# Attention state gathered in the second result bank and scaled out by VectorE

## The reference

```python
x = x + tanh(g_xattn) * mlstm(layernorm(x), ctx, ctx, Wi, bi, Wf, bf, ln_scale)
x = x + tanh(g_ffn) * moe(layernorm(x), ...)        # top 2 of 16 experts, and a shared one

def mlstm(q, k, v, Wi, bi, Wf, bf, ln_scale):       # b=16, s=256, e=512, nh=16, dh=32
    ig, fg = gates of concat([q, k, v])             # (b, nh, s, 1)
    log_f_cum = [0, cumsum(log_sigmoid(fg))]
    log_D = where(ltr, log_f_cum[1:] - log_f_cum[1:].T, -inf) + ig.T
    max_log_D = max(log_D, axis=-1)
    D = exp(log_D - max_log_D)
    C = (q @ k.T / sqrt(dh)) * D
    normalizer = maximum(abs(C.sum(-1)), exp(-max_log_D))
    h = (C / (normalizer + 1e-6)) @ v
    return (h - mean(h)) * rsqrt(var(h) + 1e-6) * ln_scale      # per head of 32
```

## Time and profile before

| | |
|---|---|
| median of 3 runs | 920.21 us (920.08 to 920.5) |
| the profiled execution | 923.91 us, of which the span of the instructions 922.2 us |
| PE busy | 740.1 us, 80% of the span |
| DVE, POOL, ACT busy | 571.1, 441.7, 410.6 us |
| attention stage | from about 106 us to 340 us of the span |

### The profile page before, as it was taken

The page is one execution under the profiler, slowest core; times in us unless marked ns, Lnnn a source line. Parts: engine busy times, 40 slices in busy tenths (PEclk is TensorE's granted clock), DMA queues, the critical chain, the costliest instruction groups (busy, mean ns, idle before and its releaser), DMA issues.

```text
span 922.2 us, 21232 instructions
## 1 busy us (share of the span) xinstructions
PE 740.1 (80%) x7464; PEld 631.7 (68%) x7464; DVE 571.1 (62%) x1144; ACT 410.6 (45%) x817; POOL 441.7 (48%) x652
## 2 busy tenths in 40 slices
PE   1772399999999947802999979999999999698892
PEld 1441167667666636602999969999999998697881
DVE  4763556766766769687556645565565554575765
ACT  1764256666666634531222225565656655212110
POOL 2111247777777751153888851111112112677884
PEclk9987579999999977955999999999999999899997
DMA  8861454543543219002341034777767745334342
GB/s 274 262 230 32 138 170 133 162 121 129 160 130 124 85 54 390 17 1 93 150 161 58 0 111 142 246 233 237 246 217 253 238 141 186 108 118 160 114 140 78
DMA packets 91311, 139.31 MB, mean 151 GB/s; under 512 B 17322, under 2 KB 44714, under 8 KB 91264
## 3 DMA queue, kind: packets, MB, share of 16 engines
q1 hardware_dynamic: 71648, 111.41, 36.6%
q0 software_dynamic: 10240, 16.82, 5.7%
q10 hardware_dynamic: 9376, 10.49, 3.5%
HBM read 103.66 MB, written 43.38 MB: 159 GB/s over the span
## 4 chain that ended last, share of the span: by engine, by line
PE 33%; POOL 12%; issue 5%; DVE 2%; ACT 1%; DMA 1%; POOLq 0%; DVEq 0%; ACTq 0%
PE f_psH L1301 21%; PE f_psY L1323 10%; POOL w13l L1575 3%; POOL w13h L1575 3%; PE f_psT L1278 3%; POOL f_hl L1557 2%; POOL disp L1565 2%; POOL idle L1552 1%; DVE xres L1475 1%; DMA yexp<-ystage 1%; DVE f_xrows L1411 0%; DVE f_xl L1427 0%; ACT f_xh L1347 0%; DVE w2l L1434 0%; DVE f_w2l L1434 0%
## 5 line engine op out<-in xcount | busy, mean ns | idle before, releaser
L1557 POOL TENSOR_TENSOR f_hl<-f_hh 128x256 fp32r<-128x256 f32 (+1 forms) x96 | 73.9, 777 | 197.5 <-ACT f_hh L1365 197.0
L1301 PE MATMUL f_psH<-f_xh,f_w13h 128*128 128x256 f32 (+1 forms) x384 | 111.4, 290 | 2.7 <-DVE f_xl L1427 2.4
L1301 PE MATMUL f_psH<-f_xh,w13h 128*128 128x256 f32 (+1 forms) x384 | 109.9, 286 | 2.4 <-DVE f_xl L1427 2.4
L1301 PE MATMUL f_psH<-f_xh,f_w13l 128*128 128x256 f32 (+1 forms) x384 | 110.1, 287 | 0.0
L1301 PE MATMUL f_psH<-f_xl,f_w13h 128*128 128x256 f32 (+1 forms) x384 | 109.8, 286 | 0.0
L1301 PE MATMUL f_psH<-f_xh,w13l 128*128 128x256 f32 (+1 forms) x384 | 108.8, 283 | 0.0
L1301 PE MATMUL f_psH<-f_xl,w13h 128*128 128x256 f32 (+1 forms) x384 | 108.5, 283 | 0.0
L1360 ACT ACTIVATE f_sg<-f_psH 128x256 f32<-128x256 f32 (+1 forms) x96 | 36.1, 379 | 152.5 <-PE f_psH L1301 141.7
L738 ACT ACTIVATE dec<-ring 128x512 f32<-128x512 f32 x128 | 76.5, 597 | 45.4 <-PE ring L645 41.8
L1365 ACT ACTIVATE f_hh<-f_hh 128x256 fp32r<-128x256 f32 (+1 forms) x96 | 39.6, 413 | 113.5 <-DVE f_hh L1447 113.2
L1447 DVE TENSOR_TENSOR f_hh<-f_sg,f_psH 128x256 f32<-128x256 f32 (+1 forms) x96 | 39.4, 415 | 78.9 <-ACT f_sg L1360 70.0
(11 more groups left out here) (221 smaller groups left out, 1920.2 us busy)
## 6 DMA issues: line engine op xcount, KB each, us to landing
raw<-w13T SPq DMA_DIRECT2D x64, 352.0 KB, 3.9
gcT<-ctxT ACTq DMA_DIRECT2D x8, 1024.0 KB, 6.7
kT<-ctxT SPq DMA_DIRECT2D x16, 512.0 KB, 5.4
qst<-qT_all SPq DMA_DIRECT2D x16, 512.0 KB, 6.2
ctxs<-ctx SPq DMA_DIRECT2D x16, 512.0 KB, 3.4
disp<-zeros SPq DMA_DIRECT2D x4, 2048.0 KB, 17.6
raw<-w2T SPq DMA_DIRECT2D x16, 512.0 KB, 4.2
f_xrows<-disp SPq DMA_DIRECT2D x16, 512.0 KB, 5.1
```

The costliest lines, as they stand in the source:

```text
L1301: last = nc.tensor.matmul(psH[m][0:n, v, :], w[wp][:, c, col:col + n], x[xp][:, c, :], start=(c == 0 and p == 0), stop=(c == DC - 1 and p ...
L1557: nc.gpsimd.tensor_tensor(hs[r % 2][1][0:n, m, :], hh[0:n, m, :], hs[r % 2][0][0:n, m, :].bitcast(F32), ALU.subtract).then_inc(s["hl_ready ...
```

## The change

The state no longer goes through a ring bank. `gather_state` writes it to psO's second bank, columns 264 to 391, beside the results, and stands between D2 and D3 in place of behind `values`; it waits for `o_taken` of the result two steps back. VectorE copies and scales it out (four instructions, `keep_state`), between `take` and `residual` of the even step ahead of it, and counts up `state_taken`, for which `back` waits. ScalarE has no `keep_state`, and its `root` stands behind `keep_output` in place of ahead of it. The ring has 20 uses in a loop round where it had 22, and its bank turns are new: in an odd step D0 of the next step now follows D3's bank, and not that of `values`. GpSimd's `keys` waits for the new counter, and its `lift_values` of first chunks now waits by itself for the `values` that read them.

```diff
-        USES = 22
-        FIRST = (2, 6, 12, 17, 23, 28, 34)
-        LAST2, OUT, STATE = 0, 2, 3
+        USES = 20
+        FIRST = (2, 6, 11, 16, 21, 26, 31)
+        LAST2, OUT = 0, 2
 
         def next2(r):
-            return 3 + r % 2 if r > 0 else 2
+            return 3 if r > 0 else 2
...
-            def gather_state(i, r, out):
+            def gather_state(i, r):
                 b = batch(i, r)
                 pe.wait_ge(kk_ready, b + 1)
                 pe.wait_ge(v_ready, 2 * b + 1)
+                if r >= 2:
+                    pe.wait_ge(o_taken, 4 * i + r - 1)
                 for gg in range(4):
                     for k in range(4):
                         h = 4 * gg + k
-                        last = nc.tensor.matmul(out[32 * k:32 * k + 32, gg * DH:(gg + 1) * DH], kkw[:, h, :],
+                        last = nc.tensor.matmul(psO[32 * k:32 * k + 32, 1, 264 + gg * DH:264 + (gg + 1) * DH], kkw[:, h, :],
                                                 vals[:, 0, h, :], start=True, stop=True)
-                last.then_inc(filled, 1)
+                last.then_inc(state_done, 1)
 
             def back(i, r, out_use):
...
+                pe.wait_ge(state_taken, batch(i, r) + 1)
...
                     decay(i, r, 2 + k, bank(r, LAST2 + k))
+                    if r % 2 == 1 and k == 0:
+                        gather_state(i, r)
...
-                if r % 2 == 1:
-                    ring_free(use(STATE))
-                    gather_state(i, r, bank(r, STATE))
...
-                pe.wait_ge(emptied, uses(i, r, STATE) + 1)
-                values(i, r, bank(r, STATE + 1))
-                back(i, r, uses(i, r, STATE + 1))
+                pe.wait_ge(emptied, uses(i, r, OUT))
+                values(i, r, bank(r, OUT + 1))
+                back(i, r, uses(i, r, OUT + 1))
...
+                if r >= 1:
+                    keep_output(use(OUT), bank(r, OUT))
                 if r >= 2:
                     root(i, r - 2)
-                if r >= 1:
-                    keep_output(use(OUT), bank(r, OUT))
-                if r % 2 == 1:
-                    keep_state(use(STATE), bank(r, STATE))
...
+            def keep_state(i, r):
+                b = batch(i, r)
+                dve.wait_ge(state_done, b + 1)
+                if r >= 2:
+                    dve.wait_ge(inter_done, b)
+                for k in range(4):
+                    last = nc.vector.tensor_scalar(state[32 * k:32 * k + 32, :, k, :],
+                                                   psO[32 * k:32 * k + 32, 1, 264:264 + DC * DH].rearrange("p (g e) -> p g e", e=DH),
+                                                   SCALE, None, ALU.mult)
+                last.then_inc(state_taken, 1)
...
                 if r >= 1:
                     take(i, r - 1)
+                if r % 2 == 0:
+                    keep_state(i, r + 1)
                 if r >= 2:
                     residual(i, r - 2)
...
                 if r >= 2:
-                    pool.wait_ge(filled, uses(i, r - 1, STATE) + 1)
+                    pool.wait_ge(state_done, b)
...
-                if c == 1 and r >= 2:
-                    pool.wait_ge(filled, uses(i, r, OUT) + 1)
+                if r >= 2:
+                    pool.wait_ge(filled, uses(i, r if c == 1 else r - 1, OUT) + 1)
```

More of the change, by code:

```diff
@@ L536, in attention_stage @@
         (filled, emptied, v_ready, qk_done, c_done, inter_done, back_done, sq_ready, o_taken, red_done, ve_ready,
-         x_done, t_ready, kk_ready, qsc_ready, state_zero, weights_set, y_ready, chain, pch, ach) = map(
+         x_done, t_ready, kk_ready, qsc_ready, weights_set, y_ready, state_done, state_taken, chain, pch, ach) = map(
             a.sem, ["at_" + n for n in (
                 "filled", "emptied", "v_ready", "qk_done", "c_done", "inter_done", "back_done", "sq_ready", "o_taken",
-                "red_done", "ve_ready", "x_done", "t_ready", "kk_ready", "qsc_ready", "state_zero", "weights_set", "y_ready", "chain",
+                "red_done", "ve_ready", "x_done", "t_ready", "kk_ready", "qsc_ready", "weights_set", "y_ready", "state_done",
+                "state_taken", "chain",
                 "pool", "act")])
@@ L743, in keep_output @@
                 nc.scalar.activation(outT[:, :, :].rearrange("p c t -> p (c t)"), src[:, :], ACT.Copy).then_inc(emptied, 1)
[L745 to L751, removed]
             def square(i, r):
@@ L786, in drain @@
             def drain(i, r):
-                keep_output(uses(i, r, STATE + 1), bank(r, STATE + 1))
+                keep_output(uses(i, r, OUT + 1), bank(r, OUT + 1))
                 root(i, r - 1)
@@ L794, in _ @@
                 exps(0, k, k, ring[k])
-            act.wait_ge(state_zero, 1)
             run(act, c_, 4, step, drain)
@@ L836, in residual @@
                                         ALU.add).then_inc(x_done, 1)
-            nc.vector.memset(state[:, :, :, :], 0.0).then_inc(state_zero, 1)
+            def keep_state(i, r):
[8 more added lines that the diff above has]
+                last.then_inc(state_taken, 1)
+            c_.link(nc.vector.memset(state[:, :, :, :], 0.0))
             c_.link(nc.vector.tensor_scalar(g.coef[:, :], g.coef[:, :], (2.0 / CELL_EPS) ** 0.5, None, ALU.mult))
```

## The result

The changed kernel takes 930.29 us (median of 4 runs, 929.59 to 933.42), the one before 920.36 us in the same rounds: a ratio of 1.0103, 95% interval 1.0068 to 1.0138. By the ratio it is slower by about 9.5 us (the two medians are 9.9 apart), where +6.7 us and 926.9 were forecast. The time lies 0.3 us over the upper end of my wide range, 917 to 930, and 0.8 over that of the likeliest case, 924.5 to 929.5.

A forecast was written before the change was run, and what follows sets the result against it. PE was busiest (80% of the span), but after the change VectorE was to set the odd step: 5.7 us from fourteen odd steps plus 1.0 at the end, +6.7 on 920.2, giving 926.9 us; range 917 to 930.

The forecast's parts named there:

- wide range: Whole kernel: 917 to 930 us, meant to hold the measured time in 8 of 10 cases.
- likeliest case: Odd steps: keys blocks residual and VectorE's weigh delays the next queries; 926.9 us, own range 924.5 to 929.5, chance 0.62.
- TensorE's gain: Odd step: PE alone would reach its next queries at 208.24, not 208.53; 0.29 us less each, 4.1 us in all.
- The copies: VectorE's four state copies ahead of residual take 0.8 to 1.2 us, making residual ready between 204.98 and 205.38.
- The collision: Odd step: residual waits for GpSimd's whole keys instruction, ending 0.54 us after it; next queries 0.41 us later than before.
- Residual shows 1.1 to 1.5 us: Expected profile sign: residual's length in steps that follow a copy, in place of 0.69 us.
- 14 x 0.41: Odd steps 3 to 29: fourteen, each 0.41 us longer, together +5.7 us.
- The end: Last step, 31: residual ready 0.8 to 1.2 us later, weigh with it, about +1.0 us into the drain.
- In the forecast both give the same sum: VectorE's copies: whether they take 1.2 us without overlap or 0.8 us with it, the forecast total is the same.
- Rival 1: Odd step: residual goes before keys, no collision, PE sets the step; -3.1 us, 917.1 us, chance 0.18.
- Rivals 2 and 3: 2: no collision but slow copies, about 921 us, chance 0.12; 3: residual misses its turn behind L899, 941 us, 0.04.
- Rival 4: Odd step: the change does not free D0, PE gains nothing, forecast stands; only Rival 1 becomes +1; no separate chance given.

The follow-up runs named there:

- the second run: The changed kernel, but GpSimd's keys waits until VectorE's residual of the same step is done; 926.39 us, ratio 1.0027.
- the masked one: The changed kernel with one VectorE instruction, multiplying by a 128x4 mask, in place of the four copies; 921.33 us, ratio 0.9984.

## Why the prediction was right

The mechanism was right and is shown; the size was too small, +6.7 us against +9.5.

- **TensorE's gain.** An odd step of 6.21 us was measured where nothing else holds it; 208.24 - 201.93 = 6.31 was forecast. The gather moved D3 by 0.39 us and not by 0.48. The 0.48 is the time from its first start to its last end, not the room that it takes. This had no effect on the forecast, since VectorE set the step.
- **The copies.** They started 0.30 us apart and took 1.19 together, by the upper bound. They began 2.17 to 2.26 us after the queries, against 2.25 forecast.
- **The collision.** Inside a round keys started at 2.84 us against 2.90 forecast, residual ended 0.55 behind it against 0.54, and the odd step was 7.00 us, +0.40 against +0.41. This is the step of the forecast on which the sign hung, and the second run shows it: without the collision the odd steps are 6.5 us shorter in all. "Residual shows 1.1 to 1.5 us" holds at the seam (1.37) and not inside (0.96), where residual started only 0.41 us before keys ended. At the seam the forecast had some luck. It did not know that keys starts at 3.17 us there, and its own lower bound for the copies would have had residual ready at 3.05 (204.98), ahead of keys. As it was, keys led by 0.23 us.
- **What failed in size: the fourteen alike.** "14 x 0.41" took one odd step for all. In half of them keys stands first in the loop's round, and in GpSimd's program the loop's branch is just ahead of it. Keys starts 0.33 us later there, and this goes straight through the blocked residual to TensorE: 7.33 us in 6 of the 7 and 7.18 in step 3, where the loop is entered. That makes +7.82 in place of +5.7. That the 0.33 us are the branch's is read from its place; no run moved the branch. The order of GpSimd's program shows the branch there, and I looked at one step. The gaps of before would not have told it: keys waited for the gather anyway, and its gap is 0.77 us inside a round and 0.80 at the seam:

```profile
219.65 1.05 POOL L890 TENSOR_TENSOR kkw<-ctxs,tmE 128x512 f32<-128x512 f32 x1 [0.80 <-PE ring L685]
```

- **The end.** It cost +1.29 against +1.0. Residual was ready 1.2 later, the upper end of my 0.8 to 1.2, and weigh started 0.03 behind residual's end where it had started 0.08 ahead of it. "In the forecast both give the same sum" was wrong here: copies of 1.2 us cost 0.4 more at the end than copies of 0.8, and I had put the middle.
- **Rivals.** Rival 1 needed residual first. The same-partition copies and the masked one at the seam show that case, with odd steps of 6.21 us. Its "copies 0.20 apart" were right for copies on the same partitions. Rivals 2 and 3 did not occur. Rival 4 did not either, since D0 no longer waits for outT.

## What to carry to other kernels

Whether work given to an engine with room is free depends on where it stands. It was free in a place where the engine had waited (the copies amid the weigh, -0.7%), and it was not free ahead of the instruction that others wait for (+1.0%). When a transfer of work frees another engine's start, look at what that engine then does at that moment, and whether VectorE's next instruction reads two SBUF operands while GpSimd does. And read a repeated step at every place where the code differs, the loop's seam first: what a wait has hidden there comes out when the wait goes.

## What the runs showed of the hardware that I had not expected

- A blocked instruction pays for the other's rest even where the lead is small: 0.05 us of lead cost 0.86 us (1.55 against 0.69), and the step was 6.87 us in place of 6.21.
- Behind the overlapping copies a GpSimd instruction that started 0.43 us before residual was held until residual's end. Behind the masked instruction one that started 0.05 before it was not. At what moment VectorE gets its turn is left open; I can name none that fits both runs.
- Residual starts at partition 0 and follows a copy that starts at 96. It started 0.03 us behind the copies' end in the changed kernel, and 0.06 ahead of it where all copies are on partitions 0 to 31. The first weigh behind residual, the next to read PSUM, started 0.03 behind residual's end in the first case and 0.07 ahead of it in the second.
- Step 1, in which TensorE's granted clock rises from 1.2 to 2.4 GHz, took 7.75 us in the run with residual first and 9.63 in the one in which keys waits for residual. Up to the end of that step the two programs are the same, and the last weigh of the step ended 7.40 us after the queries in both; but from 119 to 122 us the granted clock was 0.79 in the first and 0.50 in the second. Over all profiles the step took 7.75 to 9.97 us. So some 2 us between two single profiles can come from there and not from an edit.
